# Gated units of an audio tower: one product for queries and keys, five transfers for its rows, and a written table of PSUM banks

## The reference

```python
h = tok(x)                                   # conv (3 taps) -> q, k, v; elu; softmax attention; L = 748 rows
h = h + gated(layernorm(h)); h = h + moe(layernorm(h))

# gated:
h = layer_norm(x) @ expand                   # 128 -> q 16, k 16, linear 256, pre_gelu 256
gated = linear * gelu(pre_gelu)              # first half is "local", second half are the values v
logits = q @ k.T / sqrt(16) + mask           # causal, with a bias by distance
out = x + concat([local, softmax(logits) @ v]) @ project
# moe: router (64 experts, top 2, capacity 128), one shared FFN 128 -> 512 -> 128, weighted by the gate
```

## Time and profile before

| | |
|---|---|
| median of 3 runs | 804.29 us (804.16 to 804.44) |
| the profiled execution | 804.39 us, its span 802.7 us (1.7 us lie around the span) |
| PE busy | 778.9 us, 97% of the span |
| DVE, ACT, POOL busy | 674.7, 504.3, 288.6 us (84%, 63%, 36%) |
| mean granted TensorE clock | 0.994 |

### The profile page before, as it was taken

How to read it: one execution, slowest core, us unless ns; L and a number is a source line. 1 busy time by engine, 2 the same in 40 slices (tenths; PEclk the granted TensorE clock), 3 DMA queues, 4 the chain that set the end, 5 groups by cost and what they waited for, 6 DMA issues and landing times. The chain is left out here.

```text
span 802.7 us, 15609 instructions
## 1 busy us (share of the span) xinstructions
PE 778.9 (97%) x5555; PEld 475.5 (59%) x5555; DVE 674.7 (84%) x1608; ACT 504.3 (63%) x1100; POOL 288.6 (36%) x291
## 2 busy tenths in 40 slices
PE   9899999999999999999999999999999999999997
PEld 5354564564564564564563343367878788787785
DVE  3797998999899899899899889648788887787956
ACT  3275776776777677677677677655554636546333
POOL 4355241241342342342644245312436342333222
PEclk9799999999999999999999999999999999999999
DMA  4509143143143145135125300010000000000001
GB/s 112 78 18 122 11 61 85 15 62 84 15 63 83 15 57 88 15 53 92 16 44 81 67 7 5 9 14 8 2 21 1 20 20 2 21 1 20 20 2 38
DMA packets 85676, 31.08 MB, mean 39 GB/s; under 512 B 58496, under 2 KB 84320, under 8 KB 85600
## 3 DMA queue, kind: packets, MB, share of 16 engines
q1 hardware_dynamic: 85024, 29.61, 22.4%
q10 hardware_dynamic: 576, 0.49, 0.4%
HBM read 4.76 MB, written 3.06 MB: 10 GB/s over the span
## 5 line engine op out<-in xcount | busy, mean ns | idle before, releaser
L464 ACT ACTIVATE probs<-ps_a 128x384 f32<-128x384 f32 (+1 forms) x732 | 301.0, 480 | 129.1 <-PE ps_a L668 126.7
L552 DVE TENSOR_REDUCE neg_max<-ps_a 128x1 f32<-128x512 f32 (+1 forms) x384 | 247.9, 677 | 39.6 <-PE ps_a L684 36.1
L668 PE MATMUL ps_a<-q_rep,k_rep 98*128 98x384 bf16 (+3 forms) x768 | 231.8, 324 | 1.7 <-DMA q_rep<-max_T 1.0
L684 PE MATMUL ps_a<-k_rep,q_rep 96*128 96x512 bf16 (+3 forms) x768 | 218.3, 327 | 8.0 <-DVE neg_max L552 4.9
L699 PE MATMUL ps_pv<-probs,v_hat 128*32 128x364 f32 (+3 forms) x1536 | 135.6, 482 | 1.2 <-DVE out_r L531 0.6
L668 PEld LDWEIGHTS ps_a<-q_rep,k_rep 98*128 98x128 bf16 (+1 forms) x768 | 77.3, 102 | 94.9 <-issue 37.7
L684 PEld LDWEIGHTS ps_a<-k_rep,q_rep 96*128 96x128 bf16 (+1 forms) x768 | 75.1, 103 | 86.9 <-DVE neg_max L552 27.0
L554 DVE TENSOR_REDUCE neg_max<-ps_a 128x2 f32<-128x472 f32 x192 | 122.7, 639 | 0.0
L699 PEld LDWEIGHTS ps_pv<-probs,v_hat 128*32 128x32 f32 (+1 forms) x1536 | 42.7, 109 | 60.9 <-issue 40.5
L2009 POOL TENSOR_TENSOR out_n<-out_r,inv_sum 128x192 f32<-128x192 f32 x32 | 16.3, 511 | 157.4 <-DVE inv_sum L533 149.2
L279 POOL TENSOR_SCALAR qk_e<-qk_e 128x748 f32<-128x748 f32 x14 | 38.0, 2714 | 25.7 <-ACT qk_e L370 25.7
(11 more groups left out here) (239 smaller groups left out, 1182.3 us busy)
## 6 DMA issues: line engine op xcount, KB each, us to landing
k_rep<-parts_k SPq DMA_DIRECT2D x96, 96.0 KB, 3.8
q_rep<-parts_q SPq DMA_DIRECT2D x93, 96.0 KB, 4.0
hall<-out_n SPq DMA_DIRECT2D x256, 12.0 KB, 1.8
xT<-in_x SPq DMA_DIRECT2D x8, 375.0 KB, 3.7
out_h<-y_out SPq DMA_DIRECT2D x7, 320.0 KB
q_rep<-max_T SPq DMA_DIRECT2D x32, 6.0 KB
w_sb<-in_w_T SPq DMA_DIRECT2D x2, 256.0 KB, 3.5
out_h<-y_out SPq DMA_DIRECT2D x8, 54.0 KB
```

Of the source, the lines that this page charges most:

```text
L464: act.activation(probs[0:rows(kt), n % RING, 0:w], ps_a[0:rows(kt), 3 + n % 3, 0:w], ACT.Exp, scale=DH ** -0.5).then_inc(p_ready, 1)
L552: dve.tensor_reduce(neg_max[0:rows(t), 0, col:col + 1], ps_a[0:rows(t), c, :], AX.X, ALU.max, negate=True).then_inc(sc_max, 1)
L668: pe.matmul(out[0:rows(kt), 0:QW[qh]], k_rep[0:KM, cb % 2, h, kt * P:kt * P + rows(kt)], q_rep[0:KM, cb % 2, qh, h, 0:QW[qh]], start=True, ...
L684: last = pe.matmul(out, q_rep[0:KS, it % 2, t // QT, h, t % QT * P:t % QT * P + rows(t)], k_rep[0:KS, it % 2, h, 512:L] if c == 2 else k_r ...
```

## The change

1. Queries and keys of units 1 to 7 come from one product. `qk(n)` uses `qk_w3`, 3 x 16 columns of queries and 3 x 16 of keys; `high`, `left`, `middle`, `rest` run once on 96 rows with the factors `take_3`, and `rest` writes to `part_a[:, 1]` and not to `qk_rep`.
2. `qk_rep` has two buffers. SP fills it in five transfers a unit (`spread_qk`), two after `high`, three after `rest`; `scores` of a unit waits for `x_spread`.
3. Other places: on PE `qk` stands ahead of `scores_T` 0 (for unit 1, between the tiles 2 and 3 of `attend`), on ACT `high` behind exponential 0 and `middle` behind exponential 3, on DVE `left` behind `weigh` 0 and `rest` behind `weigh` 4.
4. Banks are named in a table, `FIRST_UNIT` for unit 0 and `LATER_UNITS` for all other iterations, the last ones too.
5. The last quarter of the token attention's outputs is turned at the start of the second block's DVE program (`turn_outputs`), not at the end of the first's.
6. POOL makes 8 small constants more in the first block, DVE 2 small copies.

```diff
+        def spread_qk(n):
+            def move(j, at, src):
+                sp.dma_start(qk_rep[at:at + src.shape[0], n % 2, j, 0:L], src).then_inc(S["x_spread"], 16)
+            if n > 1:
+                sp.wait_ge(S["y_st"], (n - 1) * NT)
+            sp.wait_ge(S["x_part_a"], n)
+            move(0, 0, part_a[0:3 * QK, 0, :])
+            move(1, 5 * QK, part_a[5 * QK:6 * QK, 0, :])
+            sp.wait_ge(S["x_last"], n)
+            move(0, 3 * QK, part_a[0:3 * QK, 1, :])
+            move(1, 0, part_a[3 * QK:6 * QK, 1, :])
+            move(1, 3 * QK, part_a[3 * QK:5 * QK, 1, :])
...
         for it in range(B + 1):
             if it >= 2:
                 store(it - 2)
+            if 0 < it < B:
+                G["rows_of_max"](sp, it)
             if it == 0:
                 spread(sp, B - 1, 0)
+            if it + 1 < B:
+                spread_qk(it + 1)
+            if it == 0:
                 spread(sp, B - 1, 1)
-            elif it < B:
-                G["rows_of_max"](sp, it)
...
     def scores(pe, o, n, t):
-        if t == 0:
-            pe.wait_ge(S["x_rep"], n * 2 + 2)
+        if t == 0 and n == 0:
+            pe.wait_ge(S["x_rep"], 2)
+        elif t == 0:
+            pe.wait_ge(S["x_spread"], 80 * n)
...
-        def high(n, j):
-            act.wait_ge(S["x_qk"], n * 2 + j - 1)
-            act.copy(in_two(part_a[:, j, :]), halves("qk", n, j)[0:KS]).then_inc(S["x_part_a"], 1)
+        def high(n):
+            act.wait_ge(S["x_qk"], n)
+            if n > 1:
+                act.wait_ge(S["x_spread"], 80 * (n - 1))
+            act.copy(in_two(part_a[:, 0, :]), halves("qk", n)[0:KS]).then_inc(S["x_part_a"], 1)
...
-        def rest(n, j):
-            dve.wait_ge(S["x_part_b"], n * 2 + j - 1)
-            dve.scalar_tensor_tensor(qk_rep[0:KS, j, 0:L], part_b[:, j, :], take_out[:, j, 1:2], left_a[:, j, :],
-                                     ALU.mult, ALU.add).then_inc(S["x_rep"], 1)
+        def rest(n):
+            dve.wait_ge(S["x_part_b"], n)
+            dve.scalar_tensor_tensor(part_a[:, 1, :], part_b[:, 0, :], take_3[:, 1:2], left_a[:, 0, :],
+                                     ALU.mult, ALU.add).then_inc(S["x_last"], 1)
...
+LATER_UNITS = {("local", 0): 4, ("values", 0): 6, ("values", 1): 2, ("scores", 0): 0, ("scores", 1): 1, ("scores", 2): 7,
+               ("local", 1): 4, ("ffn2", 2): 6, ("turn3", 0): 2, ("turn2", 0): 0, ("scores", 3): 6, ("scores", 4): 4,
+               ("scores", 5): 2, ("logits", 0): 7, ("ffn1", 0): 0, ("ffn1", 1): 4, ("turn_max", 0): 6, ("ffn1", 2): 2,
+               ("ffn1", 3): 0, ("qk", 0): 4, ("scores_T", 0): 2, ("ranks", 0): 7, ("scores_T", 1): 0, ("scores_T", 2): 6,
+               ("ffn2", 0): 2, ("scores_T", 3): 3, ("scores_T", 4): 7, ("scores_T", 5): 6, ("attend", 0): 4,
+               ("ffn2", 1): 2, ("turn_att", 0): 6, ("project", 0): 0}
...
 def places():
-    at, bank = {}, 0
-    for it in range(-1, B + 2):
+    at = {}
+    for it in range(B + 2):
         for name, unit, i, banks in order_of(it):
-            if bank + banks > 8:
-                bank = 0
-            at[name, unit, i] = (bank, banks)
-            bank = (bank + banks) % 8
+            at[name, unit, i] = ((LATER_UNITS if it else FIRST_UNIT)[name, i], banks)
     return at
...
     @block.vector
     def _(dve):
+        turn_outputs(dve, ps_pv, B - 1, 3)
         dve.memset(table[:, :], 0.0).then_inc(setup, 1)
```

More of the change, by code:

```diff
@@ L860, in _ @@
             last_step(s, probs_step(B, s))
+    return ps_pv
 QK = 16
@@ L996, in constants @@
                 select(take_out[:, n, which:which + 1], ALU.is_ge, fill, term * QK - 1, -1, 0)
+        step(pool.memset(take_3[:, :], 0.0))
+        for which, edges in ((0, ((0, -1.0), (3, 0.0), (4, -1.0))), (1, ((2, -1.0), (3, 0.0), (5, -1.0)))):
+            for term, fill in edges:
+                select(take_3[:, which:which + 1], ALU.is_ge, fill, term * QK - 1, -1, 0)
         step(pool.iota(expert_i[:, :], pattern=[[1, NE]], base=0, channel_multiplier=0))
         step(pool.tensor_copy(expert[:, :], expert_i[:, :]))
-        step(pool.memset(qk_rep[KS:KM, 1, :], 1.0))
+        for i in range(2):
+            step(pool.memset(qk_rep[KS:KM, i, 1, :], 1.0))
         step(pool.memset(nmax[:, :], 0.0))
@@ L1124, in scores @@
             diag = b == w
-            last = pe.matmul(o[0:rows(t), a:b], qk_rep[0:KS, 0, t * P:t * P + rows(t)], qk_rep[0:KS, 1, a:b],
+            last = pe.matmul(o[0:rows(t), a:b], qk_rep[0:KS, n % 2, 0, t * P:t * P + rows(t)], qk_rep[0:KS, n % 2, 1, a:b],
                              start=True, stop=not diag)
@@ L1251, in gated_units @@
     nx2T, part_a, left_a, part_b, qk_rep = (G[n] for n in "nx2T part_a left_a part_b qk_rep".split())
+    qk_w3, take_3 = (G[n] for n in "qk_w3 take_3".split())
     gel = sb("gel", [P, NT, P], F32)
@@ L1481, in _ @@
         turned_2(1)
-        for j in range(2):
-            high(1, j)
+        high(1)
+        middle(1)
         turned_att(0)
-        for j in range(2):
-            middle(1, j)
         for it in range(1, B + 1):
@@ L1512, in _ @@
                     exponential(it, k)
-            if x:
-                high(it + 1, 0)
-                high(it + 1, 1)
+                    if x and k == 0:
+                        high(it + 1)
+                    if x and k == 3:
+                        middle(it + 1)
             if z:
@@ L1519, in _ @@
                 act.activation(table[:, 1:2], table[:, 0:1], ACT.Gelu)
-            if x:
-                middle(it + 1, 0)
-                middle(it + 1, 1)
             if y:
@@ L1703, in _ @@
                     local(it, j)
+                left(it + 1)
+                attended(it)
+                rest(it + 1)
                 G["normalise"](dve, it + 2)
-                attended(it)
-                for j in range(2):
-                    left(it + 1, j)
-                for j in range(2):
-                    rest(it + 1, j)
                 sum_2(it)
@@ L1736, in _ @@
                     weigh(it, k)
+                    if x and k == 0:
+                        left(it + 1)
+                    if x and k == 4:
+                        rest(it + 1)
             if z and it < B:
@@ L1746, in _ @@
                 probabilities(it - 1)
-            if x:
-                left(it + 1, 0)
-                left(it + 1, 1)
             if y:
@@ L1753, in _ @@
                 transform(it - 1, 1)
-            if x:
-                rest(it + 1, 0)
-                rest(it + 1, 1)
             if z and it < B:
@@ L1791, in turn_2, with qk @@
             turn(o, nx2).then_inc(S["x_turned"], 1)
-        def qk(n, j):
-            o = take("qk", n, j, "x_left", n * 2 + j - 1)
-            if j == 0:
-                pe.wait_ge(S["x_nx2T"], n + 1)
+        def qk(n):
+            o = take("qk", n, 0, "x_left", n)
+            pe.wait_ge(S["x_nx2T"], n + 1)
             for h in range(2):
-                last = pe.matmul(o[0:KS, 512 * h:512 * h + HALF], qk_w[:, j, :, :].rearrange("p a c -> p (a c)"),
+                last = pe.matmul(o[0:KS, 512 * h:512 * h + HALF], qk_w3[:, :, :, :].rearrange("p j a c -> p (j a c)"),
                                  nx2T[:, h * HALF:(h + 1) * HALF], start=True, stop=True)
@@ L1834, in scores_T @@
                 diag = a == 0
-                last = pe.matmul(o[0:rows(k), a:b], qk_rep[0:KM, 1, k * P:k * P + rows(k)], qk_rep[0:KM, 0, k * P + a:k * P + b],
+                last = pe.matmul(o[0:rows(k), a:b], qk_rep[0:KM, n % 2, 1, k * P:k * P + rows(k)], qk_rep[0:KM, n % 2, 0, k * P + a:k * P + b],
                                  start=True, stop=not diag)
@@ L1840, in scores_T, with attend @@
             last.then_inc(S["y_st"], 1)
-        def attend(n):
+        def attend(n, between=None):
             o = take("attend", n, 0, "y_norm", n + 1)
@@ L1845, in attend @@
             for t in range(NT):
+                if between and t == 3:
+                    between()
                 pe.wait_ge(S["y_p"], n * NT + t + 1)
@@ L1924, in _ @@
         turn_2(1)
-        attend(0)
-        for j in range(2):
-            qk(1, j)
+        attend(0, lambda: qk(1))
         turn_att(0)
@@ L1956, in _ @@
                 ffn1(it - 1, 3)
+            if x:
+                qk(it + 1)
             if y:
```

84 lines of the change are left out of this document (42 added, 42 removed).

## The result

The changed kernel takes 806.66 us (median of 7 runs, 806.28 to 809.77), the kernel before in the same session 804.29 (803.91 to 804.44): ratio 1.0041, 95% interval 1.0026 to 1.0056. The change costs 2.4 us, and the forecast was 806.6. In a later session, in 6 and 11 runs, the same two kernels took 808.71 and 804.01 (ratio 1.0050, 1.0031 to 1.0068).

What follows compares the result with a forecast made beforehand. PE, 97% busy, was taken to bound the middle units, with the exponentials' chain close behind, POOL's chain last around unit 2 and DVE in the tail. Terms summed to -2.25 against 804.39, giving 806.6 us, range 802.9 to 809.5.

Steps and rivals of the forecast that it cites:

- border and unit 0: Start of the second block: +0.9 from DVE's moved turn, +0.3 as unit 0's one product moves into attend.
- units 1, 2, 3: -0.4 by contention on POOL's chain, -1.7 by later probabilities delaying turn_3, +1.2 in unit 3, where turn_3 waits anyway.
- units 4, 5, 6: Middle units: each gains 0.35, not 1.28, after waits for a bank, an exponential and weighings; +1.05 together.
- unit 7: No product to save: 0.43 for scores 2, 1.5 for ffn2 0 with about half back; together -1.2.
- tail: Last unit: ffn2 1 shares bank 2 with ffn2 0 and waits for its read on DVE; -2.4.
- the 1.28 that the product is worth: On PE, one of two qk products goes per unit in units 0 to 6; 1.28 us if PE alone bound.
- the 2 to 3 that I had named as a sign: Sign of the forecast: turn_3 of unit 3 would wait 2 to 3 us for the norm.
- The rival with the clock: Tail: PE's idle time drops its clock to half, up to 3.7 us more, 808 to 810.3; chance 0.12.
- The transfers: SP's five transfers a unit: covered, cost 0; without cover up to 2 us.
- The first block's additions: Copies and constants of the first block: cost 0, at most 0.3, as POOL is idle for most of it.
- The chances: Whole kernel: faster 0.14, same 0.24, slower 0.62, with borders 802.7 and 805.9; about 0.13 below the range.
- PE keeps what it saves: Rival: left and rest fit between weighings, units 0 to 6 give up to 9.0, time 798.1; chance 0.14 below 802.7.

Runs made afterwards that it cites:

- no_border: The changed kernel with the last turn of the outputs back at the end of the first block; 808.56 us, ratio 1.0051.
- scores_bank: The kernel of tail_bank with scores 2 in bank 3 and not in bank 7 beside values 0; 805.01 us, ratio 1.0025.
- tail_bank: The changed kernel with the last unit's second ffn2 product in bank 3, not in bank 2 beside the first; 804.29 us, ratio 0.9995.
- late_product: The changed kernel with qk back between scores_T 4 and 5, left and rest behind the weighings, and a bank table for that order; 801.59 us, ratio 0.9967.
- late_early_root: late_product with scores 2 of units 1 to 3 in bank 7, POOL's root earlier and residual held (units 1, 2), attended ahead of rest on DVE; 795.38 us.
- root_then_norm: tail_bank with POOL's inverse root ahead of the residual sum in units 1 and 2, the sum held until DVE has normalised; 799.65 us, ratio 0.9942.
- before_made: The kernel before the change plus only the first block's eight POOL constants and two DVE copies, which nothing reads; 803.02 us, ratio 0.9986.

## Why the prediction was right, by its own steps

The forecast of 806.6 us met 806.66. The table sets its sum beside the stretches of the traces (gains are plus). For units 1 to 3 the prediction counts from one late `turn_3` to the next, so the traces are read at the same marks: from the first `sum_2` to `turn_3` of unit 2, from there to that of unit 3, and from there to `sum_2` of unit 3.

| step | predicted | in the traces |
|---|---|---|
| border and unit 0 | +1.2 | +1.23 (from the end of the first block to the first `sum_2`, 20.30 to 19.07) |
| units 1, 2, 3 | -0.4, -1.7, +1.2 | 0.0, -1.65, +0.68 |
| units 4, 5, 6 | +0.35 each | +0.39, +0.39, +0.74 |
| unit 7 | -1.2 | -1.53 |
| tail | -2.4 | -2.3 at full clock |
| sum | -2.25 | -2.0, and -1.4 to -1.6 more where the clock falls in the tail |

The steps come out near their sizes, the largest misses being those of unit 3 (0.5) and of units 1 and 6 (0.4 each). That the whole agrees to 0.1 us is luck. In the first trace the second block and the tail lost 3.6 us, and the first block gave back 1.7 by its start, of which the prediction knew nothing; the same program had a median of 808.71 in the next session.

- *The border* is shown by no_border, 0.87 of the 0.9.
- *A middle unit* gains 0.39 of the 1.28 that the product is worth. Scores 2 wait 0.34 us, and scores_bank gives back 0.46 (0.43 predicted). `ffn2` 0 starts 0.36 us behind the last start of `scores_T` 2 in the trace of tail_bank (700.42 after 700.06) and 0.05 behind it in late_product (698.17 after 698.12): a wait of 0.31, predicted 0.30. (By the prediction's own terms it is 0.24, as 699.91 and 0.78 make 700.69 and not 700.75.) Attention is spread over 5.23 us where it had 4.96, 0.27 more. The three make 0.92, and 0.89 is missing. With the three gone, and the new wait ahead of `turn_att` too, a middle unit gives 33.08 - 31.82 = 1.26 (late_early_root), so nothing else of size is at work. Only the first was taken away by itself; the other two are read from rows.
- *Units 1 to 3*: the sum was right (-0.9, measured -0.96), and so was the mechanism in unit 2. `probabilities` end 21.95 us behind `turn_3` of that unit and not 19.63, so 2.3 later (predicted 2.5); from there to the end of the inverse root it is 12.30 us and not 12.97, so 0.7 less (predicted 0.8), as the `pow` that took 2.17 beside `rest` takes 1.51. root_then_norm gives back 1.65 and 1.72 by moving POOL's root. One wait was missing from the prediction, which had `attended` come in time: in unit 2 DVE has the statistics and the norm of later units ahead of it, and PE waits 1.47 us ahead of `turn_att`. PE therefore comes later to `turn_3` of unit 3, which waits 1.36 us and not the 2 to 3 that I had named as a sign; and `turn_3` of unit 2 waits too, 1.29.
- *Unit 6* gave 0.74 and not 0.35; its middle part has no `normalise` on DVE. No run tells whether that is the reason.
- *Unit 7* was sized too small: `ffn2` 0 waits 1.35 us for the exponential in the trace (predicted 1.5) and scores 2 wait 0.27 (predicted 0.43). A third wait, 0.34 us of scores 5 for ACT's read of `turn_3`, is a fourth pair in the table that I had not followed (both have bank 2). That makes 1.96, about what the prediction had before it took some off, and only 0.43 came back, not the 0.8 that I assumed. The row of `ffn2` 0 in unit 7:

```profile
763.30 2.05 PE L1936 MATMUL banks<-w_sb,hid 128*128 128x128 f32 x16 [1.35 <-ACT p_raw L1477]
```

- *The tail* was right as a wait (2.3 of 2.4). The rival with the clock, a chance of 0.12 in the prediction, happened on top of it in both traces of the changed kernel, at 1.4 to 1.6 us and not at its worst, 3.7. No trace tells in how many of the other runs (806.28 to 809.77) it happened.
- *The transfers* cost nothing: no trace shows `scores` 0 waiting for one. *The first block's additions* cost nothing (before_made). *The chances*: 0.14 below 802.7 and 0.13 below 802.9 don't fit together, as the second has to be the larger.
- *The rival "PE keeps what it saves"* was wrong for this order: `left` and `rest` did delay the weighings. Its price of a middle unit, 1.28, is what late_early_root shows (1.26) where they stand behind the weighings. That kernel's 795.4 is not the rival's 798.1, as it lacks the tail's loss and has POOL's chain changed.

## What to carry to other kernels

When a table of banks replaces dealing them out by turns, follow each pair of neighbours in a bank to the reader that stands between them, in every phase of the pipeline and above all in the last one, where the order on the reader's engine is different. Of an operation that moves, ask which queue it now stands in and what is behind it there: of the 1.28 us saved on PE in a middle unit, two waits for banks (0.34 and 0.31) and the pauses behind two operations on DVE (0.27) took all but 0.39, and the same two operations pushed back the end of POOL's chain in unit 2, which cost 1.65 us there. And a change of the order on one engine should be judged by its stretch in the trace, since the time of the whole moves by as much for other reasons.
